# Fp16 parts turned by DMA, fp16 output matmuls and new engine programs in a cross-attention and FFN kernel on one Trainium2 core

## The reference, cut to what matters

```python
xn = layernorm(x)                                  # over the 1024 columns
qh = softmax(Wq @ xn, over the 64 rows of a head) * 64**-0.5
kh = softmax(Wk @ ctx, over the 1024 columns)
vh = Wv @ ctx
context = kh @ vh.T                                # 64 x 64 for each head
out = Wo @ (context.T @ qh) + bo
x2 = x + out / norm(out, over the 128 rows) * g * sqrt(128)
w = dequant(qweight, scales, zeros)                # 1024 x 1024
y = x2 + layernorm(x2) @ w + bias
```

## Time and profile before

| | |
|---|---|
| median of 3 runs | 751.45 us (751.0 to 751.82) |
| profiled execution, span from first to last instruction | 750.2 us |
| its own time | not given separately; 1.25 us less than the median is the span |
| busy share PE / DVE / ACT / POOL | 95% / 81% / 59% / 53% |

### The profile page before, as it was taken

One profiled execution on the slowest core, in us unless ns is written; L12 is line 12 of the kernel. 1 busy time (PEld: TensorE's weight loads), 2 busy tenths in 40 slices (PEclk: granted clock), 3 DMA queues, 4 the chain that ended last, 5 costly groups with the idle time before them and its releaser, 6 DMA issues.

```text
span 750.2 us, 12239 instructions
## 1 busy us (share of the span) xinstructions
PE 713.0 (95%) x3895; PEld 509.6 (68%) x3895; DVE 611.3 (81%) x1041; ACT 442.3 (59%) x756; POOL 399.8 (53%) x362
## 2 busy tenths in 40 slices
PE   4879899999999999999999999999999999999776
PEld 3646767677777767677777768677676777777442
DVE  4878879898888989888898888889898988888532
ACT  3766666574666657475656747565665647575311
POOL 3251645738374574738366563837557372843542
PEclk9979999999999999999999999999999999999996
DMA  8001020301102030200203030020303020010100
GB/s 304 5 29 57 3 82 0 114 1 55 59 29 84 0 112 0 91 21 28 84 0 112 0 112 0 31 81 3 108 0 112 0 65 19 0 57 1 56 21 36
DMA packets 12022, 37.00 MB, mean 49 GB/s; under 512 B 1480, under 2 KB 3040, under 8 KB 12000
## 3 DMA queue, kind: packets, MB, share of 16 engines
q1 hardware_dynamic: 12000, 36.72, 14.3%
HBM read 28.32 MB, written 8.39 MB: 49 GB/s over the span
## 4 chain that ended last, share of the span: by engine, by line
PE 82%; DVE 6%; issue 5%; ACT 4%; POOL 1%; DMA 1%; POOLq 0%; SPq 0%; DVEq 0%; ACTq 0%
PE ps_m L844 12%; PE ps_tb L817 7%; PE ps_m L890 6%; PE ps_m L891 6%; PE ps_k L788 4%; PE ps_k L789 4%; PE ps_k L790 4%; PE ps_o L788 4%; PE ps_o L790 4%; PE ps_tb L830 4%; PE ps_q L788 4%; PE ps_o L789 4%; PE ps_q L789 4%; PE ps_q L790 3%; PE ps_ta L830 3%
## 5 line engine op out<-in xcount | busy, mean ns | idle before, releaser
L358 POOL TENSOR_TENSOR q_exp<-q_exp,q_rec 128x512 f32<-128x512 f32 x128 | 142.1, 1115 | 303.9 <-DVE q_rec L626 302.8
L463 ACT ACTIVATE q_exp<-q_exp 128x512 f32<-128x512 f32 x128 | 80.6, 630 | 79.9 <-DVE q_exp L617 76.6
L631 DVE TENSOR_TENSOR q_lo<-ps_tb,q_hi 128x512 fp32r<-128x512 f32 x128 | 88.2, 689 | 47.3 <-ACT q_hi L470 46.7
L844 PE MATMUL ps_m<-k_t,c_t 128*128 128x512 f32 x256 | 115.3, 593 | 0.9 <-ACT c_t L553 0.8
L470 ACT ACTIVATE q_hi<-ps_tb 128x512 fp32r<-128x512 f32 x128 | 76.7, 599 | 34.4 <-PE ps_tb L817 32.8
L890 PE MATMUL ps_m<-w_int,x_lo 128*128 128x512 f16 x240 | 93.2, 389 | 1.5 <-DVE x_lo L696 1.5
L458 ACT ACTIVATE k_exp<-ps_k,k_nmax 128x1024 f32<-128x1024 f32 x64 | 71.2, 1112 | 38.6 <-DVE k_nmax L605 37.9
L617 DVE TENSOR_TENSOR q_exp<-ps_q,q_nmax 128x512 f32<-128x512 f32 x128 | 88.5, 691 | 6.0
L891 PE MATMUL ps_m<-w_int,x_hi 128*128 128x512 f16 x240 | 92.5, 386 | 0.0
L623 DVE TENSOR_REDUCE q_sum<-q_exp 128x8 f32<-128x512 f32 x128 | 86.1, 673 | 1.6
L612 DVE TENSOR_REDUCE q_nmax<-ps_q 128x8 f32<-128x512 f32 x128 | 87.1, 680 | 0.1
(11 more groups left out here) (118 smaller groups left out, 1492.2 us busy)
## 6 DMA issues: line engine op xcount, KB each, us to landing
x_in<-in_x SPq DMA_DIRECT2D x16, 512.0 KB, 4.9
c_in<-in_ctx SPq DMA_DIRECT2D x16, 512.0 KB, 3.3
x_res<-in_x SPq DMA_DIRECT2D x16, 512.0 KB, 4.2
out_x<-y SPq DMA_DIRECT2D x15, 512.0 KB, 2.9
og<-in_L_ffn_qweight SPq DMA_DIRECT2D x1, 512.0 KB, 5.3
sq<-in_L_ffn_qweight SPq DMA_DIRECT2D x1, 512.0 KB, 6.2
x2b<-in_L_ffn_qweight SPq DMA_DIRECT2D x1, 512.0 KB, 7.0
x<-in_L_ffn_qweight SPq DMA_DIRECT2D x1, 512.0 KB, 8.7
```

What stands on the lines that cost most here:

```text
L358: nc.gpsimd.tensor_tensor(chunk, chunk, rec, ALU.mult).then_inc(qs_done, 1)
L631: nc.vector.tensor_tensor(q_lo[:, :, j * P:(j + 1) * P], ps_tb[:].rearrange("p (c t) -> p c t", c=HC), q_hi[:, :, j * P:(j + 1) * P].bitca ...
L844: last = nc.tensor.matmul(ps_m[:], c_t[:, t, :], k_t[:, t, :], start=(t == 0), stop=(t == TC - 1))
```

## The change

It touches every engine's program.

- Q: GpSimd scales q in pairs of chunks (1024 columns), with the reciprocal times 2^12. ScalarE writes the fp16 high part of a pair (`high_q`), GpSimd the fp16 low part (`low_q`), both still tokens by features. SyncE turns each with `dma_start_transpose` of 128 x 1024 fp16 into `q_hi` or `q_lo` (`turn_q`): eight per batch. The PE transposes L817, the moves L470 and the VectorE subtractions L631 are gone.
- X2: x2n is split in SBUF (`x2n_hi` on ScalarE, `x2n_lo` on VectorE) and turned by two more DMAs; L933, L530 and L696 are gone.
- G: its largest magnitude is found (`g_abs`, a transpose on PE by `spread_g`, `g_top`), G is brought to a range of 2^8, and g_hi, g_lo are fp16. The output matmuls are fp16, as many as before. `sq` and `og` undo the scale.
- Buffers: `c_hi`, `c_lo`, `c_t` become two each. `sum_q` runs over a pair of chunks with one more small instruction. SyncE's program is written out in full, without a loop.
- Order, by step. PE: `mix_m` goes from steps 0 and 1 of the next iteration to steps 6 and 7 of its own, `mix_g` from 2 to 0, output from 3 and 4 to 2 and 3, FFN half 0 from 4 and 5 to 1, half 1 from 6 and 7 to 4 and 5, ctx transposes from 7 to 0 and 1, column sums from 5 to 4, the spreading of `rn` from 6 to 5. The statistics of x2 and x2n are made in the same iteration (steps 6 and 7), no longer in the next.

GpSimd's new order in full: low_q(c,2) and scale_q(c,3) in step 0; low_q(c,3) and `x2b` in 1; `c_lo` and scale_q(a,0) in 2; y half 0 and low_q(a,0) in 3; scale_q(a,1), the power of x's variance and then `rn` in 4; low_q(a,1) in 5; the residual x2, scale_q(a,2) and the powers of x2's variance in 6; `xn_lo` and y half 1 in 7. ScalarE makes x2n, then high_q(a,2), then x2n_hi in step 7. In the first iterations the rows of scales go through `ps_o` instead of `ps_m`.

The diff, cut to its core:

```diff
@@ SyncE @@
+            def turn_q(b, p, parts):
+                into = slice(2 * p, 2 * p + 2)
+                for name in parts:
...
+                    sp.wait_ge(done, 4 * b + p + 1)
...
+                    sp.dma_start_transpose(turned[:, into, :, :].rearrange("p t c r -> p (t c) r"),
+                                           tok[p % 2][:]).then_inc(sems[p], 16)
...
+                if do_f:
+                    sp.wait_ge(x2hi_done, f + 1)
...
+                    sp.dma_start_transpose(x2_hi[:], x2n_hi[:]).then_inc(x2hi_turned, 16)
+                    sp.wait_ge(x2lo_done, f + 1)
+                    sp.dma_start_transpose(x2_lo[:], x2n_lo[:]).then_inc(x2lo_turned, 16)
...
+                    turn_q(c, 2, ("lo",))
...
+                    turn_q(c, 3, ("hi", "lo"))
+                    turn_q(a, 0, ("hi", "lo"))
+                    turn_q(a, 1, ("hi", "lo"))
+                    turn_q(a, 2, ("hi",))
@@ GpSimd @@
+                    if j == 0 and do_c:
+                        low_q(c, 2)
+                        scale_q(c, 3)
+                    if j == 1 and do_c:
+                        low_q(c, 3)
...
+                    if j == 2 and do_a:
+                        scale_q(a, 0)
+                    if j == 3 and do_f:
+                        add_y(0)
+                    if j == 3 and do_a:
+                        low_q(a, 0)
+                    if j == 4 and do_a:
+                        scale_q(a, 1)
...
+                        pool.wait_ge(n2_moved, c + 1)
+                        nc.gpsimd.tensor_tensor(rn[:], n2[:], neg_half[:], ALU.pow).then_inc(rn_done, 1)
+                    if j == 5 and do_a:
+                        low_q(a, 1)
...
@@ ScalarE @@
+                    if j == 1 and do_c:
+                        high_q(c, 3)
+                        act.wait_ge(gfit_steps, 5 * c + 3)
...
+                        nc.scalar.activation(g_hi[:], g_t[:], ACT.Identity, scale=g_fit[:]).then_inc(ghi_done, 1)
+                    if j in (3, 5) and do_a:
+                        high_q(a, (j - 3) // 2)
@@ VectorE @@
+                    if j == 0 and do_f:
...
+                        nc.vector.tensor_tensor(x2n_lo[:], og[:], x2n_hi[:], ALU.subtract).then_inc(x2lo_done, 1)
+                    if j == 0 and do_c:
+                        sum_q(c, 3)
...
+                        nc.vector.tensor_reduce(g_abs[:], g_t[:].rearrange("p c o -> p (c o)"), op=ALU.max, axis=AX_X,
+                                                apply_absolute_value=True).then_inc(gabs_done, 1)
+                    if j == 1 and do_c:
+                        dve.wait_ge(ghi_done, c + 1)
+                        nc.vector.scalar_tensor_tensor(out=g_lo[:], in0=g_t[:], scalar=g_fit[:], in1=g_hi[:],
+                                                       op0=ALU.mult, op1=ALU.subtract).then_inc(glo_done, 1)
+                    if j in (2, 4, 6) and do_a:
+                        sum_q(a, (j - 2) // 2)
@@ TensorE @@
+                    if j == 0 and do_c:
+                        mix_g()
+                    if j == 1 and do_c:
+                        spread_g()
+                    if j == 1 and do_f:
+                        feed_forward(0, 0, TC)
+                    if j in (2, 3) and do_c:
+                        mix_out(j - 2)
...
+                    if j in (6, 7) and do_a:
+                        mix_m(4 * (j - 6), 4 * (j - 6) + 4)
```

More of the change, by code:

```diff
@@ L95, in build @@
         xn_lo = [sb(f"xn_lo{s}", [P, N], F32R) for s in range(2)]
-        c_hi = sb("c_hi", [P, N], F32R)
-        c_lo = sb("c_lo", [P, N], F32R)
-        c_t = sb("c_t", [P, TC, P])
+        c_hi = [sb(f"c_hi{s}", [P, N], F32R) for s in range(2)]
+        c_lo = [sb(f"c_lo{s}", [P, N], F32R) for s in range(2)]
+        c_t = [sb(f"c_t{s}", [P, TC, P]) for s in range(2)]
         stats1 = sb("stats1", [P, 2, 6])
@@ L112, in build @@
         k_t = sb("k_t", [P, TC, HID])
-        q_hi = sb("q_hi", [P, HC, N], F32R)
-        q_lo = sb("q_lo", [P, HC, N], F32R)
+        q_tok_hi = [sb(f"q_tok_hi{r}", [P, 2 * HID], F16) for r in range(2)]
+        q_tok_lo = [sb(f"q_tok_lo{r}", [P, 2 * HID], F16) for r in range(2)]
+        q_hi = sb("q_hi", [P, STEPS, HC, P], F16)
+        q_lo = sb("q_lo", [P, STEPS, HC, P], F16)
         m_t = sb("m_t", [P, HID])
         g_t = sb("g_t", [P, HC, P])
-        g_hi = sb("g_hi", [P, HC, P], F32R)
-        g_lo = sb("g_lo", [P, HC, P], F32R)
+        g_abs = sb("g_abs", [P, 1])
+        g_top = sb("g_top", [P, 1])
+        g_unit = sb("g_unit", [P, 1])
+        g_fit = sb("g_fit", [P, 1])
+        g_undo = sb("g_undo", [P, 1])
+        gs_undo = sb("gs_undo", [P, 1])
+        g_hi = sb("g_hi", [P, HC, P], F16)
+        g_lo = sb("g_lo", [P, HC, P], F16)
         og = sb("og", [P, N])
@@ L328, in iteration @@
                         sp.dma_start(halves(out[f])[h], halves(y)[h]).then_inc(y_stored, 16)
[L329 to L336, removed]
+            for i in range(FIRST, LAST):
+                iteration(i, i % 2, 0 <= i < NB, 0 <= i - 1 < NB, 0 <= i - 2 < NB)
             sp.wait_ge(y_stored, 16 * (NB + 1))
@@ L389, in iteration @@
[L389 to L397, removed]
@@ new lines, in iteration @@
+                    if j == 3 and do_f:
+                        dve.wait_ge(x2n_done, f + 1)
+                        nc.vector.tensor_scalar(nrs2[:], rs2[:], -1.0, None, ALU.mult).then_inc(nrs_done, 1)
+                        dve.wait_ge(nrs_done, f + 1)
+                        dve.wait_ge(x2b_done, f + 1)
+                        nc.vector.scalar_tensor_tensor(out=x2b[:], in0=zero_bc[:], scalar=nrs2[:], in1=x2b[:],
+                                                       op0=ALU.mult, op1=ALU.add).then_inc(x2c_done, 1)
@@ L860, in mix_g, with spread_g, mix_out @@
                     last.then_inc(g_ready, 1)
[L862 to L865 removed]
+                def spread_g():
+                    pe.wait_ge(gabs_done, c + 1)
+                    nc.tensor.transpose(ps_o[1][:, 0:P], g_abs[:].to_broadcast([P, P]), ident[:]).then_inc(gabs_ready, 1)
+                def mix_out(h):
+                    if h == 0:
                         pe.wait_ge(ghi_done, c + 1)
                         pe.wait_ge(glo_done, c + 1)
[L868 to L871 removed]
+                    for p in (2 * h, 2 * h + 1):
+                        pe.wait_ge(qhi_turned[p], 16 * (c + 1))
+                        pe.wait_ge(qlo_turned[p], 16 * (c + 1))
+                    tok = slice(4 * h, 4 * h + 4)
+                    ps = ps_o[h][:].rearrange("p (t r) -> p t r", t=4)
+                    for fc in range(HC):
+                        last = three(ps, g_hi[:, fc, :], g_lo[:, fc, :], q_hi[:, tok, fc, :], q_lo[:, tok, fc, :],
                                      start=(fc == 0), stop=(fc == HC - 1))
[L873 to L874 removed]
+                    last.then_inc(out_ready, 1)
                 def feed_forward(h, k0, k1):
```

507 lines of the change are left out of this document (238 added, 269 removed).

## The result

The changed kernel takes 783.28 us (median of 4 runs, 782.84 to 783.83), the kernel before 751.25 beside it: ratio 1.0423 [1.0408, 1.0437], slower. The profiled execution has a span of 781.7 us at a mean granted clock of 0.972 (before 750.2 and 0.983). The page: busy times, and the chain that ended last.

A forecast was written before the change was run, and what follows sets the result against it. PE bound the kernel before; then a loop through DVE, ACT, POOL and PE would: 41.9 us plus 3.55 of collisions, 45.5 per iteration. 750.2 + 14 x 2.45 + 1.25 gave 786 us, range 688 to 835.

The forecast's parts named there:

- The 14 middle iterations: Iterations 2 to 15: each forecast at 45.5 us, 2.45 more than before.
- PE's demand: PE's own work per middle iteration after removed transposes and fp16 output matmuls: 38.6 us, down from 43.05.
- Costs on the other engines: Work per iteration: POOL 34.5 us, DVE about 33.5, ACT near 27; none alone over PE's 38.6.
- The chain: Loop from k's projection through DVE, ACT, POOL and PE to the next iteration: 41.9 us before collisions.
- the waits named as signs: PE waits expected: rn about 3 us, g_lo before output about 2, g_abs before spread_g about 2.
- Collisions: DVE waits for POOL on x2n_lo 0.85, g_lo 1.9, L715 (x2b) 0.8: sum 3.55 us per iteration.
- DMAs at 0: Ten 256 KB transposes per iteration on SyncE's queue: hidden up to 5 us each, costed at 0 in the middle.
- Iteration 1: The iteration without FFN: chain 40.8 us against 40.4 before, so no change.
- the 6: Head and tail together: forecast at 0, plus or minus 6 us.
- Rival 1: Lock waits do not fall on the chain: 41.9 us per iteration, 735 us; chance 0.23.
- Rival 2: PE stays the bound in the middle: 38.6 us per iteration, 686 us; chance 0.17.
- Rival 3: PE's clock falls to 1.2 GHz for half the mix_m stretch: 48.9 us per iteration, 833 us; chance 0.11.
- Rival 4: DMA transposes bind, 5.6 us each without overlap: 948 us; chance 0.09, including anything over it.

The follow-up runs named there:

- experiment 10: On experiment 9: x_hi and x_lo transposes issued first, high_q(c,2) behind k_exp(0), scale_q(c,3) waiting for DVE's small steps; 723.84 us.
- experiment 2: Changed kernel with g_hi ahead of high_q(c,3) on ACT; 753.5 us.
- experiment 8: On experiment 2: DVE's statistics of the next batch moved ahead of x2b, and x2b with them behind scale_q(a,0); 748.2 us.
- experiment 1: Changed kernel with one added wait: POOL's low_q(c,3) also waits until g_lo is done; 764.01 us.
- experiment 5: Changed kernel with q turned by DMA for the first batch only, 120 of 128 q transposes left out; 786.67 us.
- experiment 9: On experiment 8: q's pair 3 sum into step 7, x2n_lo ahead of shift_q(0), x2n_hi and m_t ahead of high_q(c,2); 773.33 us.
- experiment 4: On experiment 3: POOL's scale_q(a,1) also waits until xn is done; 809.37 us.
- experiment 3: Changed kernel with rn ahead of ve, rstd and scale_q(a,1) on POOL; 795.12 us.
- experiment 6: On experiment 2: c_hi and c_lo made in step 0 instead of step 2; 762.44 us.
- experiment 7: On experiment 6: rn first, scale_q held for xn, low_q(a,1) behind residual adds, scale_q(a,2) behind xn_lo, high_q(a,2) next iteration; 780.04 us.

## Why the prediction was right

786 us were forecast and 783.28 measured, and the period came out at 45.05 where 45.5 stood. The mechanism was right; that the total came within 3 us is in part luck. The 14 middle iterations were to bring 34.3 us and the rest nothing. Iterations 2 to 14 brought 24.6, and what was put at nothing brought the rest of the 31.5: head 2.5, iteration 1 4.0, and 0.3 for iteration 15 and the tail together. The middle was put about 9 us too high, the head and iteration 1 6.5 us too low. By its steps:

- **PE's demand** was put at 38.6; PE is busy 39.46 us per iteration in the changed kernel and 39.26 in experiment 10. It was put 0.7 to 0.9 too low, and it is not what decides.
- **Costs on the other engines.** POOL 34.5 was too high: a low part takes 2.13 us, not 2.35, and a scaled pair 1.90, not 2.05; busy 31.8. DVE 33.5 before collisions, 36.64 with them, and the difference is near the 3.55 of the collisions.
- **The chain.** From k's projection (368.89) g_lo starts at 15.2 us (384.13); the steps gave 14.5, with x2n_lo's wait of 0.85 behind them 15.35. rn's spreading starts at 36.25 (405.14); the steps gave 32.6 and 3.55, 36.15. From there it takes 8.8 us to the next projection, against 9.3. That the loop closes over DVE, ACT and POOL is confirmed by experiment 2, where a step of ACT moved the whole period. Of the waits named as signs, the one for rn was put at 3 us and is 1.80, those for g_lo and g_abs at about 2 and are 1.72 and 1.44; the one for m_t (0.62) was not foreseen.
- **Collisions.** x2n_lo was put at 0.85 and met 0.4 (1.70 in the mean, 1.28 alone, as experiment 10 has it). g_lo was put at 1.9 over 0.7 and met 1.36. x2b was put at 0.8 and met 1.3 in the mean (2.60 against 1.28), 1.6 in the iteration read. Sum 3.1 instead of 3.55: each size was off by about half a microsecond and the errors partly cancel. Counted in full, as the forecast did, x2b's is too dear: experiment 8 takes 1.03 off it and the period falls by 0.44, with a new collision of 0.6 beside it. That g_lo is the surest one was right, and experiment 1 prices it at 19.3 us.
- **DMAs at 0** was right for this order: for q's by experiment 5, for x2's by the rows, with less room than I gave them. PE's wait ends with x_lo's landing, 0.2 us behind g_abs, and PE then still waits 1.7 us for g_lo; in the tail x_lo's landing ends a wait of 12.97 us. What I had not listed is the time on SyncE's queue, 1.23 to 1.33 us for each, which experiment 9 shows to be able to bind.
- **Iteration 1** was put at no change and took 44.46 instead of 40.43 us, at a granted clock of 0.87. This step failed: it was costed without the clock. Of its 44.46 us, 10.2 ran at 1.2 GHz, with PE idle for 7.05. In experiment 10 PE is idle for 6.54 us of iteration 1, none of it runs at 1.2 GHz, and it takes 39.0. Across the runs its length follows the time at 1.2 GHz: 39.0 and 39.3 us with none, 41.2 with 3.4 us of it, 41.8 and 41.9 with 6.8, 43.8 to 44.8 with 10.2 or more (but 42.0 in experiment 9). The head and the tail stayed inside the 6.
- **Rival 1** (locks off the chain, 735) was wrong, since the order fixes who wins: g_lo's duration in 16 iterations has a mean of 2.12. **Rival 2** (PE the bound) was wrong for this order and nearly right for the work: experiment 10 comes within 1.8 us per iteration of it. **Rival 3** did not happen in the middle (clock 1.00 from iteration 2 to 15), but it did in iteration 1 and in experiment 4, where it cost 2.1 us per iteration against the 3.4 put on it. **Rival 4** did not happen.

So the slowdown is not in what the change adds. Most of it, 29.8 of 32.0 us, is in two instructions' order on ACT, and the removed PE work pays when the order lets it.

## What to carry to other kernels

When the work of a leading engine is removed, the time can come to be set by a loop through the others, as here. Write that loop down with its queue positions, and add the collisions of DVE and POOL: ask for each pair with one common releaser which of the two starts first, and let the short one on the chain win, by order rather than by a wait. After each move read the timelines again, for small instructions too; in experiments 3, 4, 6, 7, 8 and 9 a freed collision, a wait taken away or an idle stretch filled was followed by another instruction, queue or transfer that was late next. And part a slower run into waits and granted clock before explaining it: in experiment 4 the middle lost nothing to waits and 2.1 us per iteration to the clock.

## What the runs showed of the hardware that I had not expected

- The lock also catches a tensor_scalar with one full SBUF operand (xn, 2.38 us against 0.81) and very small ones (16 columns: 2.09 against 0.17; one column: 1.10 against 0.16). The reductions, statistics and reciprocals of the middle stayed within 0.07 us of their shortest in the traces of the changed kernel and of all experiments. The Trainium skill (SBUF — State Buffer, section Who interferes with whom) lists tensor_scalar among the operations that can take the pair, and the rows of xn and q_rec agree.
- A DMA transpose of 128x1024 in two-byte elements (eight 128x128 blocks) held SP's queue for 1.23 to 1.34 us in 156 of 160 cases of the changed kernel (at most 1.63) and landed 3.0 to 3.4 us after issue in 145 of them (at most 4.8). The Trainium skill (VectorE: DVE Perf Modes, section The three transpose paths) gives 1309 ns for one block of 128x128; these times do not add up over the eight blocks here, which would be 10.5 us by an estimate from that figure.
- PE's granted clock did not follow the sum of the waits: with 5.59 us of them per iteration, none over 1.81, the middle of the changed kernel ran at 1.00 throughout; with 5.49 us, among them one of 3.6, experiment 4 spent 5.7 us of each iteration at 1.2 GHz. In experiment 9 the longest wait of the middle was 2.2 us and the clock fell too; in experiment 3 it was 1.8, as in the changed kernel, and 1.1 us per iteration ran at 1.2 GHz. What decides between these was not tested.
